# One block for the merge of heads, the first norm and the feed-forward, and a reordered prologue of the first attention

## What is computed

```python
x = L0_attn_x                                             # (2, 512, 512)
x = _layernorm(x + _L0_attn_ref(x, ...), axis=-1)         # 128 heads of 4, latent 64, rope part 64
x = _layernorm(x + _L0_ffn_ref(x, ...), axis=-1)          # silu(h1) * h3, hidden 1376, low-rank parts of 16
x = _layernorm(x + _L1_attn_ref(x, ...), axis=-1)         # 32 heads of 128, 8 key heads, causal
x = _layernorm(x + _L1_ffn_ref(x, ...), axis=-1)          # 512 x 512, rows and columns selected by clusters
...
def _L0_attn_ref(x, Wq_down, Wq_up, Wq_rope, Wkv_down, Wk_up, Wv_up, Wk_rope, Wo):
    c_q = x @ Wq_down
    c_kv = x @ Wkv_down
    q_c = (c_q @ Wq_up).reshape(b, s, N_HEADS, HEAD_DIM)
    q_r = (x @ Wq_rope).reshape(b, s, N_HEADS, ROPE)
    k_c = (c_kv @ Wk_up).reshape(b, s, N_HEADS, HEAD_DIM)
    v_c = (c_kv @ Wv_up).reshape(b, s, N_HEADS, HEAD_DIM)
    k_r = x @ Wk_rope
    scores = (jnp.einsum('bqhd,bkhd->bhqk', q_c, k_c) + jnp.einsum('bqhd,bkd->bhqk', q_r, k_r)) / scale
    attn = jax.nn.softmax(scores, axis=-1)
    out = jnp.einsum('bhqk,bkhd->bqhd', attn, v_c)
    return out.reshape(b, s, N_HEADS * HEAD_DIM) @ Wo
```

## Time and profile before

| | us |
|---|---|
| median of 3 runs (2557.84 to 2561.74) | 2560.16 |
| the profiled execution | 2563.6 |
| its span | 2561.8 |
| prologue up to the first score | 73.35 |
| from the end of the attention to the first projection of the feed-forward | 1394.2 to 1451.5 |

### The profile page before, as it was taken

The page is one execution under the profiler, slowest core; times in us unless marked ns, Lnnn a source line. Parts: engine busy times, 40 slices in busy tenths (PEclk is TensorE's granted clock), DMA queues, the critical chain, the costliest instruction groups (busy, mean ns, idle before and its releaser), DMA issues. The chain is left out here.

```text
span 2561.8 us, 40544 instructions
## 1 busy us (share of the span) xinstructions
PE 2479.7 (97%) x12630; PEld 1865.5 (73%) x12630; DVE 1560.0 (61%) x2779; ACT 1391.2 (54%) x2147; POOL 1146.3 (45%) x1146
## 2 busy tenths in 40 slices
PE   8999999999999999999998899899999999999997
PEld 3677777777777777777774588777877877878774
DVE  6566666666666666666663522375756657557556
ACT  3677777777777777777775332232423424324231
POOL 3456555555555565555553233243434335234210
PEclk8899999999999999999998999999999999999998
DMA  6222222222222222222222222111001010010001
GB/s 202 50 44 52 47 53 50 46 52 47 57 44 52 46 53 48 49 52 46 58 44 78 89 87 87 70 38 42 16 25 41 0 41 16 25 41 16 1 1 53
DMA packets 47613, 125.40 MB, mean 49 GB/s; under 512 B 6034, under 2 KB 23442, under 8 KB 41427
## 3 DMA queue, kind: packets, MB, share of 16 engines
q1 hardware_dynamic: 47570, 124.85, 18.2%
HBM read 80.27 MB, written 10.49 MB: 35 GB/s over the span
## 5 line engine op out<-in xcount | busy, mean ns | idle before, releaser
L440 DVE TENSOR_REDUCE row_max<-ps_max 128x1 f32<-128x512 f32 x1024 | 670.7, 687 | 192.4 <-PE ps_max L529 170.6
L294 POOL TENSOR_TENSOR p_parts<-probs,p_parts 128x1024 f16<-128x1024 f32 x256 | 547.7, 2149 | 360.7 <-ACT p_parts L361 360.4
L356 ACT ACTIVATE probs<-ps_score 128x1024 f32<-128x1024 f32 x512 | 523.2, 1022 | 240.8 <-PE ps_score L545 219.8
L543 PE MATMUL ps_score<-Q,K 128*128 128x512 f32 x1024 | 407.8, 398 | 1.6 <-ACT probs L356 1.6
L545 PE MATMUL ps_score<-Q,K 97*128 97x512 f32 x1024 | 407.4, 398 | 0.0
L529 PE MATMUL ps_max<-KX,Q 68*128 68x512 f32 x1024 | 379.5, 412 | 5.0 <-DMA Q<-content_q 1.8
L434 DVE TENSOR_TENSOR Q<-ps_x,Q 64x512 fp32r<-64x512 f32 x254 | 175.2, 690 | 252.9 <-ACT Q L351 249.2
L361 ACT ACTIVATE p_parts<-probs 128x1024 f16<-128x1024 f32 x256 | 269.4, 1052 | 4.0
L529 PEld LDWEIGHTS ps_max<-KX,Q 68*128 68x128 f32 x1024 | 189.2, 190 | 81.1 <-issue 35.2
L543 PEld LDWEIGHTS ps_score<-Q,K 128*128 128x128 f32 x1024 | 194.4, 190 | 59.5 <-ACT probs L356 13.4
L1328 POOL CAST q_hi<-roped 128x512 fp32r<-128x512 f32 x64 | 39.1, 610 | 415.5 <-DVE roped L1448 198.9
(11 more groups left out here) (262 smaller groups left out, 4441.7 us busy)
## 6 DMA issues: line engine op xcount, KB each, us to landing
Q<-Q SPq DMA_DIRECT2D x64, 512.0 KB, 4.3
ffn_raw<-in_w_ffn SPq DMA_DIRECT2D x22, 768.0 KB, 4.4
w_raw<-in_w_qrope SPq DMA_DIRECT2D x32, 512.0 KB, 3.6
wq_raw<-in_wq SPq DMA_DIRECT2D x8, 1024.0 KB, 5.6
wo_raw<-in_wo SPq DMA_DIRECT2D x8, 1024.0 KB, 4.8
content_k<-probs SPq DMA_DIRECT2D x8, 512.0 KB, 5.8
Q<-content_q SPq DMA_DIRECT2D x64, 64.0 KB
K<-content_k SPq DMA_DIRECT2D x64, 64.0 KB
```

The lines of the kernel that those rows point to most:

```text
L294: pool.tensor_tensor(p_lo[:, j, :, :], probs[:, j, 0:PAIRED, :], p_hi[:, j, :, :], ALU.subtract)\
L356: act.activation(probs[:, j, 2 * half:2 * half + 2, :], ps_score[half][:, :, :], ACT.Exp, scale=SCALE).then_inc(exped, 1)
L440: dve.tensor_reduce(row_max[:, t, j:j + 1], ps_max[t % 2][:, :], axis=AXX, op=ALU.max)\
L543: pe.matmul(ps_score[half][:, k, :], K1[:, b, t * P:(t + 1) * P], Q1[:, b, j, :], start=True, stop=False)
```

## The change

1. **Prologue.** The zero and one rows of Q2 and K2 are set by six VectorE memsets (four of 64x2048, two of 1x2048), ahead of the split of x; the zero and one tiles and the GpSimd copies are gone. ScalarE takes the first 9 jobs before it rounds the first rope weights. SP issues `store(0)` alone ahead of the loads of rows, and `store(1)` to `store(3)` behind them. Behind each of the eight pairs of `first_max` stands now: a quarter of the second r job (pairs 0 to 3), a third of the queries of unit 1 (pairs 4 to 6, which stood in the body as p0, p1, p2), the first v job (pair 7). The other seven v jobs stand behind T of the first unit, on TensorE, and behind A, on ScalarE. The second `rope_keys` stands behind all 16 maxima.
2. **Last unit.** SP loads the output weights there, into the first four tiles of V, which is kept until the feed-forward is done.
3. **One block.** Merge, norm and feed-forward share one block. The norm is done tile by tile: behind the count of tile t follow its mean and variance, the low part of the turned tile t-1, the reciprocal and the normalisation. TensorE turns the normalised tile t-1 behind the merge of tile t; tile 7 is turned behind the 12 low-rank products. The low-rank low parts on VectorE stand behind tiles 3 (two of them), 4, 5 and 6. The table loads stand at the start of the block (square root) and ahead of the low-rank part (Silu).

```diff
@@ mla_stage, bank(n): PSUM banks of the jobs
-            k = n % 8 if n < N_R else n % 4
+            k = n % 8 if n < N_R else n - N_R + 2 if n < N_V else (n - N_V) % 3
@@ SP
             store(0)
-            store(1)
             sp.wait_ge(parts_out[0], 64)
-            sp.wait_ge(zeros_set, 2)
-            sp.wait_ge(rows_set, 4)
+            sp.wait_ge(zeros_set, 4)
             for b in range(NB):
                 max_keys(0, b)
                 content(0, b)
-            store(2)
-            store(3)
+            for m in range(1, DC):
+                store(m)
...
+                    if last and b == 1:
+                        sp.wait_ge(v_in, 2 * n)
+                        sp.dma_start(V[:, 0:DC, :], dram["wo0"].rearrange("(c p) n -> p c n", p=P)).then_inc(sb["wo0_in"], 16)
@@ ScalarE
-            for n in range(N_R):
+            for n in range(N_R // 2):
                 job(n)
-            job(N_R)
+            act.wait_ge(w_in, 16)
+            for pair in range(2):
+                act.activation(w_hi[:, :, pair, :], w_raw[:, :, pair, :], ACT.Copy).then_inc(w_step, 1)
+            for n in range(N_R // 2, N_R + 1):
+                job(n)
...
+                        if kind == "A" and not before:
+                            for t in range(1, TT):
+                                if t == 6:
+                                    act.wait_ge(job_made, len(jobs))
+                                job(N_V + t)
@@ VectorE
+            for b in range(NB):
+                for tile in (Q2, K2):
+                    dve.memset(tile[ROPE:P, b, :, :].bitcast(F32), 0.0).then_inc(zeros_set, 1)
+            dve.wait_ge(zeros_set, 2 * NB)
+            for b in range(NB):
+                dve.memset(K2[MROW:MROW + 1, b, :, :].bitcast(F32), 1.0).then_inc(zeros_set, 1)
@@ the new swiglu_stage, VectorE
+            for t in range(TT):
+                if t % ST == 0:
+                    dve.wait_ge(x_in[t // ST], 16)
+                dve.wait_ge(y_made, t + 1)
+                dve.tensor_tensor(X[:, t, :], y_banks[t % 2][:, :], x[:, t, :], ALU.add).then_inc(y_taken, 1)
+                dve.wait_ge(y_taken, t + 1)
+                dve.bn_stats(stats[:, t, :], X[:, t, :]).then_inc(y_counted, 1)
+                dve.wait_ge(y_counted, t + 1)
+                dve.bn_aggr(moments[:, t, :], stats[:, t, :]).then_inc(mean_var, 1)
+                if t:
+                    low_x(t - 1)
+                dve.wait_ge(rooted, t + 1)
+                dve.reciprocal(dev[:, t:t + 1], dev[:, t:t + 1]).then_inc(inverse, 1)
+                dve.wait_ge(inverse, t + 1)
+                dve.tensor_scalar(X[:, t, :], X[:, t, :], moments[:, t, 0:1], dev[:, t:t + 1],
+                                  ALU.subtract, ALU.mult).then_inc(normed, 1)
+                for part in {3: (0, 1), 4: (2,), 5: (3,), 6: (4,)}.get(t, ()):
+                    swiglu_lora_low(dve, mem, part)
@@ TensorE
+            turn_o(0)
+            pe.wait_ge(wo_in, 16)
+            for t in range(TT):
+                if t + 1 < TT:
+                    turn_o(t + 1)
+                merge(t)
+                if t:
+                    turn_x(t - 1)
+            pe.wait_ge(lora_low, 5)
+            pe.wait_ge(y_taken, TT - 1)
             delta_out(0)
+            pe.wait_ge(y_taken, TT)
+            pe.wait_ge(x_low, ST)
             for s, (half, m) in enumerate(STEPS):
                 if m == 0:
                     low_rank(half)
+                if s == 0:
+                    turn_x(TT - 1)
...
```

More of the change, by code:

```diff
@@ L394, in _ @@
             job(N_R + 1)
-            for n in range(N_V, N_V + 6):
-                job(n)
-            act.wait_ge(job_made, len(jobs))
-            for n in range(N_V + 6, len(jobs)):
-                job(n)
+            job(N_V)
             for m in range(DC):
@@ L572, in turn_o, with job @@
                 last.then_inc(o_turned, 1)
-            def job(n, parts=(0, 1)):
+            def job(n, chunks=range(DC)):
                 kind, m, b = jobs[n]
-                if parts[0] == 0 and n >= 8:
-                    before = n - 8 if n < N_V else n - 4
+                if chunks[0] == 0 and n >= 8:
+                    before = n - 8 if n < N_V else N_R - 2 + n - N_V if n < N_V + 3 else n - 3
                     pe.wait_ge(job_high, before + 1)
@@ L646, in body @@
                     for kind, at in PE_ORDER:
-                        if kind == "p" and more:
+                        if kind == "p" and more and before:
                             if at[0] == 0:
@@ L995, in _ @@
         def _(sp):
+            for i in range(2):
+                half = slice(i * ST, (i + 1) * ST)
+                sp.dma_start(x[:, half, :], dram["x"].rearrange("(t p) n -> p t n", p=P)[:, half, :]).then_inc(x_in[i], 16)
+            swiglu_first_loads(sp, dram, mem)
             for s in range(RAW, NS):
```

263 lines of the change are left out of this document (123 added, 140 removed).

## The result

The changed kernel took **2536.56 us** (median of 4 runs, 2530.54 to 2540.08) where the kernel before, run beside it, took 2559.51: a ratio of 0.9912, 95% interval 0.9898 to 0.9925. That is 22.5 us less by the ratio and 22.95 by the two medians. The forecast was 2538.4 with a gain of 21.8. So the sum held. Its terms did not all hold: at the first score, where the prediction counted the prologue, it gave less than forecast in every profile, and the block gave more.

What follows compares the result with a forecast made beforehand. TensorE, busy 97% of the span, bounds the kernel; the loop was taken as unchanged. Gains of 12.3 us in the prologue and 9.5 behind the attention, 21.8 in all, took the median 2560.2 to 2538.4; 8-in-10 range 2531 to 2551.

Steps and rivals of the forecast that it cites:

- Zeros: Prologue: six VectorE memsets end at about 12.8 us, first low part at about 20.5 instead of 21.30.
- First maximum: Prologue: the DMA wait goes and the first maximum starts at 36.4 us instead of 38.57.
- The 16 maxima: Prologue: VectorE nearly the bound, from 36.4 to 50.4 us; last store landing taken at 51, at no cost.
- Turn, v jobs, first score: End of prologue: first score at 58.7 or 62.3 us, taken as 61.0, before 73.35.
- Prologue, sum: Prologue up to the first score: 12.3 us gained in all.
- Rival (a): The prologue stays at the low clock and gains nothing; second place gives 9.5 us: 2550 us, chance 0.14.
- Last unit: Last attention unit: the 1 MB weight load runs while the DMA is nearly idle and costs nothing.
- Block: Merge, norm and feed-forward up to the first projection: 9.5 us gained, range 3.8 to 11.9.
- the collision: Block: VectorE's low-rank low parts lose time beside GpSimd's weight differences; 2.4 us taken off the gain.
- (b): Block: norm by tiles drowns VectorE, four low parts each pay 2.0 us; total gain 16.1, 2544 us, chance 0.12.
- (c): Loop: a longer period, 0.43 us more in each of 62 units, makes the kernel slower: 2565 us, chance 0.04.
- (d): Both places do better: cheap memsets, full clock through v jobs, no collision; 16 + 11.9 gained, 2532 us, chance 0.06.

Runs made afterwards that it cites:

- e4_store1_between: Changed kernel with the second store issued between the two sets of row loads and the third behind them: 2534.91 us, ratio 0.9903.
- e10_wait_only: Changed kernel with only ScalarE's wait for the four stores moved behind the v jobs, to its first exponential: 2539.49 us, ratio 0.9928.
- e1_prologue_only: Only the prologue of the change; output weights, merge, norm and feed-forward as in the kernel before: 2547.04 us, ratio 0.9957.
- e0_after_again: The changed kernel itself, no edit, run again in a second session: 2541.55 us, ratio 0.9920.
- e3_weights_in_block: Changed kernel with the output weights loaded as before, at the start of the block: 2540.80 us, ratio 0.9933.
- e8_weights_first: Changed kernel with ScalarE's high parts of the feed-forward weights ahead of the root in each turn of the block's loop: 2539.39 us, ratio 0.9928.
- the three edits: Changed kernel with, each alone: second store between the row loads, 2534.91 us; memsets shared with GpSimd, 2536.08; ScalarE's store wait behind the v jobs, 2539.49.
- all three: Changed kernel with second store between the row loads, memsets shared with GpSimd, and ScalarE's store wait behind the v jobs: 2525.58 us, ratio 0.9876.
- two halves of a change: Against the kernel before: the new prologue alone, 2547.04 us; the output-weight load in the last unit with the one block alone, 2542.49 us.
- e6_both: Changed kernel with the second store between the row loads and the b = 1 memsets on GpSimd: 2533.21 us, ratio 0.9901.

## Why the prediction was right, and where its steps were not

**Zeros.** Forecast: memsets of 2.08, ending at 12.8, the first low part at 20.5. Measured: 1.76 in a row, but 2.14 from start to start (9.91, 12.05), the end at 13.81, the first low part at 21.31, exactly where it was before. The first began at 1.24, a microsecond later than I had taken it; the rate was right. The Trainium skill, page "VectorE: DVE Perf Modes", section "Zero memsets can be issued as uint32 (trn2)", counts one cycle for each element, from which the estimate of 2.13 a memset was worked out; the trace agrees with its 2.14 between starts.

**First maximum.** Forecast 36.4, measured 37.43 to 37.68. No DMA wait, as said. Of the difference 0.4 is that low part, which came no sooner. The rest goes with the clock, which was in no term: the low part stands at 21.31 in the other six profiles with these memsets too, TensorE idles 2.5 to 3.8 us ahead of its q jobs, and the granted clock then falls in all of them but one. Where it stayed at 1.00 from 22 to 28 (`e4_store1_between`) the first maximum is at 36.65; where it was at 0.50 from 22 to 28 (`e10_wait_only`) it is at 38.71.

**The 16 maxima.** Forecast: from 36.4 to 50.4 at full clock. Measured: from 37.43 to 54.60. Two things were not in the sum. VectorE's second low part stands behind the wait for the second store, which the change had moved behind the row loads; the prediction priced only the landing of the last one ("level with the maxima, so it costs nothing") and forgot that VectorE waits for each of the four on its way. And the clock went down behind that wait, so that the last pair took 2.56 (53.31 - 50.75). `e4_store1_between` shows both: without the wait the reductions end at 49.86 (47.17 + 2.69) and the clock holds. The landing itself was mis-sized as well: 55.1 to 55.8 (`e4_store1_between`, `e1_prologue_only`) and not 51, so that a quicker chain of maxima would have met it at once. (The recorded sum calls it free and still holds 0.9 us for it: 52.5 - 51.0 - 0.59.)

**Turn, v jobs, first score.** Forecast 61.0, between 58.7 warm and 62.3 cold. Measured 62.72 warm, 70.08 cold. The v jobs cost 6.27 or 12.31 behind the turn. The price of a cold one was right (1.76 each); but they stand seven in a row with nothing beside them, and I had put three of them under ScalarE's work.

**Prologue, sum.** Forecast 12.3 at the first score. Measured there: 10.6 in the changed kernel's first profile, 3.3 in `e0_after_again`, 7.1 in `e1_prologue_only`; none reaches the forecast. At the row of unit 1, by which the loop's start is set, the gains are 14.0, 4.5 and 7.9, and 13.4 and 5.5 in `e3_weights_in_block` and `e8_weights_first`, which have the same prologue. Rival (a), nothing gained, is too hard even for the cold profiles. Behind the first score the prediction had taken both kernels as alike; the warm one gained 3.4 more there (16.42 against 19.78 to the next row).

**Last unit.** The load cost nothing and saved a wait of 4.7, as said (`e3_weights_in_block`). From the last row to the first turn the profiles differ by 22.2 to 26.4 us; in the changed kernel's first one the clock was 1.00 all through. In every other profile it fell somewhere in this stretch: to a mean of 0.63 to 0.79 over the last 8 us in ten of them, and to 0.79 over the first 8 us in `e4_store1_between`. That was in no term, and I didn't test what decides it.

**Block.** Forecast 9.5, with 11.9 at best. Measured 14.7, 15.4 and 14.3. Three terms were off, all to the safe side. The first merge was kept at 5.62 in the cold and took 4.43 in one profile, with the clock at 0.50 up to 1381, and 3.70 in `e0_after_again`, with the clock at 1.00. The wait for weights alone doesn't set it: with that wait back, in `e3_weights_in_block`, it took 4.55. The tile takes 4.31 and not 4.4. And the collision, 2.4, hit GpSimd (`e8_weights_first`). VectorE is the bound by 0.83 + 0.22 us where 1.5 was said. "First projection 42 to 49 us behind the first turn": 41.79 and 41.15.

**Range and rivals.** (b), the norm drowning VectorE, did not come; `e8_weights_first` pays 2.7 of the 8 us that it had put on VectorE. (c), another period of the loop: 20.58 to 20.60 in every profile. (d) came in the block. Its 2532 was met once, by 2530.54, but not by its steps: the memsets were not at the copy's price, and the first score was at 62.72 and not at 57 to 58.

So the right total is in part luck. It rests on two errors of opposite sign: some 4 to 8 too much for the prologue in its cold executions, 5 to 6 too little for the block. The step that failed in between is that of the 16 maxima and the stores: the prediction priced the landing of the last store alone, while VectorE waited 1.56 us for the second one and the clock fell behind that wait.

## What to carry to other kernels

When transfers are moved back in a queue, list everyone who waits for each of them, not for the last alone: an engine that takes its waits in turn meets the second one on the way. And when one gap of TensorE is closed, look at once for the wait that stands next to it (here three in a chain: VectorE for the second store, ScalarE for all stores, the memsets ahead of both). None of the three edits alone showed a gain clear of the spread, the first two together still ended at the landing of the stores, and with all three the clock stayed up in the profile and the time was 11 to 16 us lower. A stretch that flips between two clocks from one execution to the next hides edits of 3 to 5 us in the total; read them between two milestones of the trace. And when two halves of a change are run alone, check that they add up to the whole: here they did not, by 5 to 7 us, and a single profile of each did not show why.

## What the runs showed of the hardware

- The same program, in two executions that agree to 0.02 us from 47.2 to 53.7 us (and to 0.25 ahead of that), got its clock back at about 54 in one and at about 75 in the other, in work that keeps TensorE busy (48 to 54: 6.00 of 6.00). The stretch was seven v jobs of 64 rows; what decided it stays open.
- GpSimd and VectorE hold each other by who starts first: a GpSimd difference of 2.40 took 3.76 when VectorE's two-input operation had started 0.09 us ahead, and a VectorE normalisation with one tile input took 2.29 and not 0.55 when GpSimd had started 0.33 us ahead. The prediction had counted on two-input operations alone. The Trainium skill, page "SBUF — State Buffer", section "Who interferes with whom", lists VectorE's tensor-scalar operation among those that can contend too, where it runs in a mode that uses both ports, and says that whichever issues first has the shared ports for the whole instruction while the other is fully blocked. The trace agrees in the main. VectorE's normalisation ended 0.3 us behind GpSimd, less than the 0.55 that it takes alone; GpSimd's 3.76 is 1.36 more than 2.40, of the 1.53 us for which VectorE's operation still ran (1404.16 to 1405.69).
- A VectorE memset of 2048 elements shows 1.76 us and comes every 2.14; for the sum the second number counts.
- GpSimd set 64x2048 in 1.80 us, 1.86 from start to start (2.69, 4.55, 6.41 in `e6_both`), where VectorE took 1.76 and 2.14, and it was idle there.
